# Matmuls without a result between the second tile's transposes, and the t3 weights split later, in a recommendation kernel

## The reference, cut to what matters

```
fm = emb_table[jnp.arange(26)[None, :], cat_idx]           # 2048 x 26 x 128, one lookup each
h = relu(dense_x @ Wd1 + bd1)                              # 13 -> 512
h = relu(h @ Wd2 + bd2)                                    # 512 -> 256
dense = relu(h @ Wdf + bdf)                                # 256 -> 128
Z = concatenate([fm, dense[:, None, :]], axis=1)           # 2048 x 27 x 128
S = einsum('bie,bje->bij', Z, Z)
x = concatenate([S[:, iu, ju], dense], axis=-1)            # pairs i < j: 351 + 128
x = relu(x @ Wt1 + bt1)                                    # t1: -> 1024
x = relu(x @ Wt2 + bt2)                                    # t2: -> 1024
x = relu(x @ Wt3 + bt3)                                    # t3: -> 512
x = relu(x @ Wt4 + bt4)                                    # t4: -> 256
return sigmoid(x @ Wo + bo)
```

## Time and profile before

| | |
|---|---|
| runs of the kernel before | 618.27, 620.19, 624.83 us |
| profiled execution, its own time | 623.32 us |
| span of its trace | 621.5 us |
| TensorE matmuls busy | 567.6 us, 91% of the span |
| TensorE weight loads busy | 535.9 us, 86% |
| VectorE busy | 212.4 us, 34% |
| ScalarE busy | 241.1 us, 39% |
| GpSimd busy | 403.1 us, 65% |
| matmuls | 8112 |
| gathers | 416 |

### The profile page before, as it was taken

The page is one execution under the profiler, slowest core; times in us unless marked ns, Lnnn a source line. Parts: engine busy times, 40 slices in busy tenths (PEclk is TensorE's granted clock), DMA queues, the critical chain, the costliest instruction groups (busy, mean ns, idle before and its releaser), DMA issues.

```text
span 621.5 us, 18061 instructions
## 1 busy us (share of the span) xinstructions
PE 567.6 (91%) x8112; PEld 535.9 (86%) x8112; DVE 212.4 (34%) x438; ACT 241.1 (39%) x506; POOL 403.1 (65%) x421
## 2 busy tenths in 40 slices
PE   0997169979799899999999999999999999999998
PEld 0775159979698899999999999999989999999997
DVE  6764434522332224322331334132413143223111
ACT  1874323523432334333443344243424243434222
POOL 5877777777777777777777777777777777200000
PEclk9999658989999999999999999999999999999999
DMA  6645737995338443674348333934376436500430
GB/s 126 169 103 112 184 54 198 316 371 130 56 53 260 119 56 54 157 224 53 57 84 292 56 55 54 305 75 55 54 215 163 56 54 169 181 3 2 146 127 0
DMA packets 35445, 77.64 MB, mean 125 GB/s; under 512 B 7990, under 2 KB 23870, under 8 KB 30582
## 3 DMA queue, kind: packets, MB, share of 16 engines
q0 software_dynamic: 13312, 27.29, 27.0%
q1 hardware_dynamic: 21496, 49.01, 22.7%
q10 hardware_dynamic: 562, 0.20, 0.2%
HBM read 68.08 MB, written 8.40 MB: 123 GB/s over the span
## 4 chain that ended last, share of the span: by engine, by line
PE 79%; POOL 13%; issue 6%; DMA 1%; DVE 1%; ACT 0%; DVEq 0%
PE acc L725 62%; POOL gathered L498 13%; PE bank L757 8%; PE unit L774 6%; PE acc L735 1%; PE unit L788 1%; DMA gathered<-table,row_of 1%; DVE feats L506 0%; DVE rows L579 0%; ACT h L633 0%; DVE h L560 0%; ACT acc L634 0%; DVE feats L505 0%; ACT h L630 0%; ACT y L639 0%
## 5 line engine op out<-in xcount | busy, mean ns | idle before, releaser
L498 POOL DMA_INDIRECT gathered<-table,row_of x416 | 402.4, 967 | 129.7 <-issue 126.5
L725 PE MATMUL acc<-h,wt 128*128 128x256 f32 (+1 forms) x2232 | 299.3, 291 | 3.6 <-issue 1.7
L725 PEld LDWEIGHTS acc<-h,wt 128*128 128x128 f32 x2232 | 279.0, 192 | 10.0 <-DVE h L560 2.5
L633 ACT ACTIVATE h<-acc,bias 128x256 fp32r<-128x256 f32 (+1 forms) x104 | 51.0, 490 | 236.9 <-PE acc L725 236.9
L560 DVE TENSOR_TENSOR h<-acc,h 128x256 fp32r<-128x256 f32 (+1 forms) x104 | 46.2, 445 | 275.3 <-ACT acc L634 263.5
L725 PEld LDWEIGHTS acc<-x,wt 126*128 126x128 f32 (+2 forms) x768 | 95.0, 195 | 4.1 <-issue 3.1
L725 PE MATMUL acc<-x,wt 126*128 126x256 f32 (+2 forms) x768 | 98.1, 288 | 0.4 <-DVE h L557 0.4
L757 PE MATMUL bank<-eye,gathered 128*128 128x128 f32 x416 | 52.7, 277 | 14.0 <-ACT feats L666 7.3
L774 PE MATMUL unit<-feats 128*27 128x26 f32 x4096 | 51.7, 194 | 10.5 <-issue 8.3
L774 PEld LDWEIGHTS unit<-feats 128*27 128x27 f32 x4096 | 43.5, 106 | 20.3 <-issue 9.2
L757 PEld LDWEIGHTS bank<-eye,gathered 128*128 128x128 f32 x416 | 46.7, 142 | 15.9 <-DMA gathered<-table,row_of 7.9
(11 more groups left out here) (46 smaller groups left out, 189.1 us busy)
## 6 DMA issues: line engine op xcount, KB each, us to landing
wt<-split_t SPq DMA_DIRECT2D x21, 1024.0 KB
raw<-w_t SPq DMA_DIRECT2D x17, 512.0 KB, 4.5
split_t<-wt SPq DMA_DIRECT2D x8, 1024.0 KB, 11.8
wt_fourth<-split_t SPq DMA_DIRECT2D x8, 1024.0 KB
gathered<-table,row_of POOLq DMA_INDIRECT x416, 3.5
raw<-w_d SPq DMA_DIRECT2D x1, 512.0 KB
feats<-xT SPq DMA_DIRECT2D x4, 104.0 KB
rows<-idx SPq DMA_DIRECT2D x1, 208.0 KB, 2.7
```

The source lines that it names most:

```text
L498: nc.gpsimd.indirect_dma_start(gathered[:, t % SLOTS, c, :], None, table, bass.IndirectOffsetOnAxis(row_of[:, t, c:c + 1], 0)).then_inc(ga ...
L633: nc.scalar.activation(parts[0], source, ACT.Relu, bias=b)
L725: mm = nc.tensor.matmul(result, strip[0:height, a, k, :], given[0:height, b, k, :], start=(n == 0 and (a, b) == (0, 0)), stop=(n == len(bl ...
```

## The change

The dictionary of pieces has t2 ahead of t3. The four t3 pieces leave `first_part` and stand in part 0's `mixed`, at places 14 to 17. SP's sequence follows the order of the pieces: after each of the first five t2 pieces' turns it writes that piece out, and it writes the last three (t2 5 to 7) after all loads. ScalarE's wait for the end of the dense network, which stood before the first t3 piece, stands before the first t2 piece; its wait for a free t2 slot holds for t2 pieces alone.

TensorE gets 34 matmuls of 512 columns whose result nobody reads: 12 behind the transposes of tile 1's group 3, 16 behind those of group 4, 6 behind those of group 5. They read weights that are split by then and write the accumulator that the next strip starts anew.

```
-PIECE = {"d2": (256, 1), "df": (128, 1), "t1": (256, 4), "t4": (256, 1), "t3": (128, 4), "t2": (128, 8)}
+PIECE = {"d2": (256, 1), "df": (128, 1), "t1": (256, 4), "t4": (256, 1), "t2": (128, 8), "t3": (128, 4)}
...
-T3_FIRST, T2_FIRST = PIECES.index(("t3", 0)), PIECES.index(("t2", 0))
+T2_FIRST = PIECES.index(("t2", 0))
...
-    early = [pieces([one]) for one in PIECES[2:T3_FIRST]]
+    early = [pieces([one]) for one in PIECES[2:T2_FIRST]]
...
-    steps += features(part, 0) + piece("t3") + features(part, 1) + regroups(part) + sum(stacks(part), [])
+    steps += features(part, 0) + features(part, 1) + regroups(part) + sum(stacks(part), [])
...
+BUSY = {3: 12, 4: 16, 5: 6}
...
         inserted += [(n, piece("t2", m)) for m, n in enumerate(places)]
+        inserted += [(14 + m, piece("t3", m)) for m in range(4)]
...
+def bottoms_done():
+
+    return SO_FAR[max(n for n in ACC_STEPS if STEPS[n][0] == "strip" and STEPS[n][2] == "df") + 1]["acc"]
...
-                if number - RAWS >= T2_FIRST:
-                    keep_t2(number - RAWS - T2_FIRST)
-            for m in range(8 - RAWS, 8):
+                if PIECES[number - RAWS] in PIECES[T2_FIRST:T2_FIRST + 8 - T2_SLOTS]:
+                    keep_t2(PIECES[number - RAWS][1])
+
+            for m in range(8 - T2_SLOTS, 8):
                 keep_t2(m)
...
-                    if number == T3_FIRST:
-
-                        act.wait_ge(acc_done, SO_FAR[at]["acc"])
-                    if number >= T2_FIRST + T2_SLOTS:
+                    if number == T2_FIRST:
+
+                        act.wait_ge(acc_done, bottoms_done())
+                    if T2_FIRST + T2_SLOTS <= number < T2_FIRST + 8:
...
                         mm.then_inc(bank_done, 1)
+                        if kind == "flip" and now["tile"] == 1 and n in BUSY:
+
+                            pe.wait_ge(acc_read, now["acc"])
+                            pe.wait_ge(low_y, now["split"])
+                            pe.wait_ge(low_w, T2_FIRST)
+                            for _ in range(BUSY[n]):
+                                nc.tensor.matmul(acc[:, now["acc"] % ACCS].rearrange("p h w -> p (h w)"),
+                                                 wt4[:, 0, 0, 0:P], wt1[:, 0, 0, 0:WIDE], start=True, stop=True)
```

## The result

The changed kernel took a median of 631.47 us (626.62 to 633.17, 4 runs), the kernel before 622.51 in the same comparison (618.27 to 628.56, 4 runs). The prediction of 619.3, with a range up to 623.3, was wrong in sign. The profiled execution of the changed kernel took 633.17 us for a span of 631.4, 9.9 more than before.

The account below looks back on a forecast made before the run. GpSimd's fixed gather pace was taken as the bound: TensorE's lead of 7.8 or 4.4 us exceeds tile 7's slack, so the gain is 3.6 us, 623.32 to 619.7 profiled; predicted median 619.3, range 616.0 to 623.3.

Parts of the forecast that it names:

- The gather bound: Tile 7: TensorE waits for its last gather, capping the gain at 3.6 us; forecast A, 616.5 to 622, chance 0.72.
- The stop at 126.87: TensorE's 3.87 us stop in a product run, read as late instructions: nothing to 5.4 us saved, 5.4 taken.
- the lead: TensorE's gain before tile 7: 4.4 + 5.4 - 2 = 7.8 us, or 4.4 if the stop stays.
- tile 7's 3.6: Slack at tile 7: its last transposes could start near 276.2, when the gather lands, instead of near 279.8.
- The case behind tile 7 (D): Behind tile 7: other late instructions where no slack covers them, 622 to 626, chance 0.05.
- TensorE's time in the first part: Up to tile 2's last flip: TensorE arrives 5.3 us earlier, near 109.1, then waits for the gather until 111.6.
- the 4.4 us: Tile 2's last gather: landed at 111.6 instead of 116.0, 4.4 us earlier (1.6 to 5.4).
- The clock: Tile 1's work, 66 to 100 us: busy matmuls hold the granted clock at 1.00, up from 0.52 over 65 to 97.
- B: Rival: clock low again at the t1 strips, only the gather's 1.5 us won, 621.8 or 619.7; chance 0.12.
- The t3 pieces: In their new place: splits between 130 and 145 us, t3 3 near 143.4, waits costing TensorE 0 to 2 us.
- Case C: Rival: t3 loads land late in the new place, no gain at 9.4 us landing, 630.7 at 11.8; chance 0.07.
- GpSimd's lengthened issues: Gather issues overlapping VectorE splits: four moved splits cost 1.6 us; tile 2's gather gains 1.5, tiles from 4 on gain 0.

Follow-up runs that it names:

- the move with 8 turns: Kernel before with only the t3 pieces moved, plus 8 tiny matmuls (32 instructions) at TensorE's start: 624.92 us, 1.0059.
- with 32: Kernel before with only the t3 pieces moved, plus 32 tiny matmuls (128 instructions) at TensorE's start: 629.19 us, 1.0149.
- shift alone: Kernel before plus 18 tiny matmuls (72 instructions) at TensorE's start, with neither moved t3 pieces nor busy matmuls: 628.28 us, 1.0124.
- kernel shifted back: Changed kernel plus 46 tiny matmuls (184 instructions) at TensorE's start, nearly a whole block from the kernel before: 622.96 us, 1.0014.
- busy matmuls alone: Kernel before plus the 34 busy matmuls, t3 pieces left in the first part: 630.08 us, 1.0146.
- move alone: Changed kernel without the 34 busy matmuls, so only the t3 pieces are moved: 621.31 us, 1.0022.
- small reads: Changed kernel with all but the first read of t2's split weights cut to 16 of 128 partitions: 623.61 us, 1.0063.
- the last kernel above: Changed kernel plus 34 tiny matmuls at TensorE's start, all but the first t2 read cut to 16 of 128 partitions: 618.92 us, 0.9956.

## Why the prediction was wrong, point by point

- **The gather bound: right as a bound.** 3.6 us at tile 7, a floor of 619.7 in the profiled execution's terms; the kernel with no stop behind 160 us came to 618.92 and waits where it was said to, and so do the move with 8 turns (276.69) and with 32 (277.13). A bound from below says only how fast it can be. The changed kernel comes to tile 7's second half at 286.07 instead of 279.03 and never meets it. I took the floor for the forecast.
- **The stop at 126.87: the step that failed.** "The 68 new ones shift where it falls" was written there, and bounded with "nothing to 5.4 us saved". I read it as late instructions, which was right, and then priced the shift as a chance of gain alone, for one stop. What it had to be bounded by is every edge behind tile 1's transposes: the 71 positions moved all of those, some 60. The sum ahead of it had a slip besides: without the stop's 5.4 and with the t3 pieces' 2 the lead is 4.4 - 2 = 2.4 us, not 4.4, and that is less than tile 7's 3.6. The case behind tile 7 (D) had a chance of 0.05 and ended at 626, on the strength of one stretch, 279 to 345, with 65.7 of 66 us busy. That stretch is quiet because of where its edges stand: with the shift alone TensorE is busy for 61.7 us of it, with the changed kernel shifted back for 65.8. What the runs showed in place of a saving is 9.4 us of stops more than before; the changed kernel is 7.0 us behind at tile 7 already, and 2.9 more go behind it.
- **TensorE's time in the first part: right only with fewer stops.** Expected at tile 2's second half at 109.1 and waiting for a gather at 111.6. The kernel shifted back has 109.82 and 111.83, with one stop of 1.66 us in tile 1's products. The changed kernel has 115.22: two stops in tile 1's products cost 4.0 us, and ScalarE waits 1.25 us for a t2 block, until 103.47. Its last two transposes of tile 2 start at 116.09, against 115.98 before: nothing of the 4.4 us was gained.
- **The clock: in between.** 0.85 from 66 to 100 us; it is low from 82.8 for 6.8 us, behind the first of those stops and through the second, and once more from 93.1 for 3.4. In the kernel shifted back it is 0.98 over the same stretch. The busy matmuls alone give 0.80 there, the move alone 0.65, so both have a part in it. The Trainium skill, "TensorE: Matmul & The Clock Gate", part 4, would have it fall in the regroup and stack transposes, as they don't count the way matmuls do; in the row of 0.98 they stand in the middle and it did not. So B is not what happened, and its 621.8 is 9.7 short of 631.5 too.
- **The t3 pieces: a small miss.** The last t3 block was split at 148.6 instead of 143.4; the loads of that time landed in up to 9.2 us. TensorE's waits there come to 1.0 us (until 141.98 and 146.20) and it was still ahead, so the price "0 to 2" stands. Case C, the slower rival, named 630.7 and the wrong cause: the move alone costs nothing (1.0022, 0.9982 to 1.0062).
- **GpSimd's lengthened issues: right at first, too small later.** Between 60 and 78 us all gathers of the changed kernel take 0.94 to 0.95. Over tiles 3 and 4 the issues are lengthened by 4.1 us in all instead of 1.8, more than the 1.6 that was put on the moved splits, and tile 7's last gather is issued at 274.51 instead of 272.66: 1.9 later, outside the "1.3 us of chance". In the twelve traces it lies between 270.86 and 274.51, so the floor itself is not fixed to better than that.

Of the 6.3 us at tile 3 a part does belong to the move. The first read of t2 goes out at 154.73 there, and at 141.78 before. Six kernels have record 3265 = 256*12 + 193 at about this place. In three of them the first read goes out between 153.8 and 155.1, and the stop there is 2.77, 3.10 and 2.76 us (changed, move alone, small reads). In the other three it goes out between 141.8 and 145.1, and the stop is 0.59, 0.33 and 0.87 (before, shift alone, busy matmuls alone). So some 2 us of the 6.3 are the read's, and the move alone has them too without being slower in all. What the late writes add stays open.

## What to carry to other kernels

Before an edit adds instructions to a long unrolled stream, look at the profile's gaps without a releaser and count their positions. If they stand a fixed number of instructions apart, any added or removed instruction ahead of them moves the whole set to new places, and the price of that can be larger than the edit's own work (here from nothing to 1.5%, and not in the order of the number of instructions); test the edit with filler at a point where the engine idles, at a few shifts, before judging it. A bound on what a lead can be worth is not a forecast of what is left.

## What the runs showed of the hardware

TensorE's instructions arrive in blocks of about 256 over the DMA engines, and every stop of 0.9 us or more that was counted in a product run or a strip, 75 in all twelve traces, is at position 193 of a block. Lengths of these are 0.9 to 3.9 us. One more idle time without a releaser, 0.65 to 1.6 us at the start of a regroup, is in all traces at no fixed position and is another matter. The stops come where the records are consumed fast (64 product matmuls in 0.74 us) and, in the woven parts, where a 1 MB read is in flight; without the reads the time is 5 to 8 us less. The Trainium skill, "Runtime: NRT & Kernel Launch", "Instruction fetch mechanics", has the blocks of 256 instructions, and the traces agree. The same section calls the cost of crossing from one to the next mostly hidden, and here it is not: nearly all of the changed kernel's 20.2 us without a releaser are such stops.

A second-order effect is the clock: with the stops at 159.4 and 164.1 it was low for 13.7 us from 161.3 on, so a stop of 2 us can cost more than itself. It need not: in the last kernel above the clock stayed at 1.00 from 67.0 us on, through a stop of 1.62 us at 79.7.

The positions in a part nearly repeat. From one part to the next TensorE has 2034 records, 14 fewer than eight blocks, so an edge stands 14 records further on in the next part's work. In the trace of the busy matmuls alone stops stand at 8385, 8641, 10433 and 10689: the second pair is 2048, eight whole blocks, behind the first. The first of each pair stands behind 31 of the 64 products of a run in one part and behind 38 in the next. So a bad edge can come back in the next part instead of averaging out.
